# Ten engine loops of a four-layer graph network written out with constants

## What is computed

```python
h = relu(layernorm(x)); x = x + L0(h)
h = relu(layernorm(x)); x = x + L1(h)
h = relu(layernorm(x)); x = x + L2(h)
h = relu(layernorm(x)); x = x + L3(h)

L0: clip(h + segment_sum(h[src] * edge_prob * weight, dst) + 0.1 * h, 0, 1)
L1: segment_sum(sum_k t[:, k] * (h[dst] @ W1[k]), src)       # 16 basis terms of edge_attr_2
L2: segment_sum(h'[src] . (edge_attr_8 @ We + be), dst) + h' @ Wr + b, and the same with the
    edges turned round; 8 + 8 columns
L3: a = segment_sum(silu(h[dst] x edge_attr_8 . Wmsg) @ Wlin, src)
    h + silu(h x a . Wupd) @ Wul
```

## Time and profile before

| | |
|---|---|
| median of 3 runs | 4584.79 us (4582.91 to 4585.53) |
| the profiled execution | 4580.59 us, span 4578.8 us |
| PE, PE's weight loads | 2142.2 us busy (47%), 1442.9 us (32%) |
| DVE | 2888.0 us (63%) |
| ACT | 1181.5 us (26%) |
| POOL | 2834.2 us (62%) |
| DMA | 319.82 MB, mean 70 GB/s |
| granted TensorE clock, mean | 0.716 |

### The profile page before, as it was taken

How to read it: one execution, slowest core, us unless ns; L and a number is a source line. 1 busy time by engine, 2 the same in 40 slices (tenths; PEclk the granted TensorE clock), 3 DMA queues, 4 the chain that set the end, 5 groups by cost and what they waited for, 6 DMA issues and landing times.

```text
span 4578.8 us, 36295 instructions
## 1 busy us (share of the span) xinstructions
PE 2142.2 (47%) x6770; PEld 1442.9 (32%) x6770; DVE 2888.0 (63%) x4329; ACT 1181.5 (26%) x2942; POOL 2834.2 (62%) x2799
## 2 busy tenths in 40 slices
PE   1200015555200005666666126666660566666998
PEld 0100014444200003333333115555550344433444
DVE  8890026666460006777777777777776688876887
ACT  1010013333310003333333234444341344431111
POOL 4877777777777776555554036555530677773776
PEclk7555557777655557888888657777775788888999
DMA  6010013333530002222224212222243233352110
GB/s 167 7 47 24 8 38 105 110 104 111 83 97 5 5 5 52 72 72 72 72 72 71 90 63 85 83 84 76 83 80 114 82 108 100 106 84 65 32 32 24
DMA packets 200402, 319.82 MB, mean 70 GB/s; under 512 B 83898, under 2 KB 166698, under 8 KB 199971
## 3 DMA queue, kind: packets, MB, share of 16 engines
q1 hardware_dynamic: 112848, 265.61, 16.3%
q0 software_dynamic: 82368, 21.64, 7.5%
q10 hardware_dynamic: 5140, 32.09, 1.8%
HBM read 66.90 MB, written 252.21 MB: 70 GB/s over the span
## 4 chain that ended last, share of the span: by engine, by line
PE 22%; DVE 19%; issue 10%; POOL 6%; DMA 2%; SPq 2%; DVEq 1%; ACT 0%; POOLq 0%
DVE work L1122 9%; PE psX L562 8%; PE psX L651 7%; POOL rows L464 5%; PE psK L553 4%; DVE psX L1152 2%; PE psX L578 2%; DVE natD L1147 2%; DMA rows<-table,rec 1%; DVEq L1122 1%; DVE work L1104 1%; SPq L407 1%; SPq L408 1%; PE psK L628 1%; DVE at_hi L1099 1%
## 5 line engine op out<-in xcount | busy, mean ns | idle before, releaser
L464 POOL DMA_INDIRECT rows<-table,rec x1792 | 1692.6, 945 | 1268.0 <-issue 528.4
L553 PE MATMUL psK<-work 128*128 128x224 f32 x3584 | 927.7, 424 | 648.8 <-DVE work L1104 374.4
L553 PEld LDWEIGHTS psK<-work 128*128 128x128 f32 x3584 | 848.1, 241 | 819.3 <-issue 501.8
L1122 DVE SCALAR_TENSOR_TENSOR work<-work,keep,psK 128x224 f32<-128x224 f32 x1792 | 799.8, 446 | 233.7 <-DVE work L1122 45.2
L562 PE MATMUL psX<-natD 128*128 128x512 f32 (+1 forms) x1120 | 682.7, 750 | 535.6 <-DVE natD L1147 257.2
L749 ACT ACTIVATE work<-iota,rec 128x128 f32<-128x128 f32 x1792 | 546.0, 391 | 641.3 <-PE psK L553 360.2
L446 POOL DMA_INDIRECT edges_by_dst<-natD,pos x391 | 440.4, 1126 | 184.1 <-issue 126.7
L562 PEld LDWEIGHTS psX<-natD 128*128 128x128 f32 x1120 | 258.0, 254 | 800.1 <-DVE natD L1147 329.7
L446 POOL DMA_INDIRECT edges_by_src<-natS,pos x391 | 403.5, 1032 | 127.2 <-issue 127.2
L1104 DVE TENSOR_TENSOR work<-at_hi,psX 128x1792 f32<-128x1792 f32 x224 | 452.3, 2019 | 6.1 <-ACT psX L791 0.3
L589 PE MATMUL psX<-ident,rows 128*128 128x128 f32 x168 | 51.9, 309 | 803.9 <-DMA rows<-table,rec 803.9
(11 more groups left out here) (142 smaller groups left out, 2068.0 us busy)
## 6 DMA issues: line engine op xcount, KB each, us to landing
scan<-work SPq DMA_DIRECT2D x224, 896.0 KB, 3.6
rows<-table,rec POOLq DMA_INDIRECT x1792
table<-h ACTq DMA_DIRECT2D x28, 896.0 KB, 3.6
work<-scan SPq DMA_DIRECT2D x168, 112.0 KB, 2.0
rec<-edges_by_dst SPq DMA_DIRECT2D x112, 84.0 KB, 1.9
natD<-scan SPq DMA_DIRECT2D x56, 112.0 KB, 2.0
edges_by_dst<-natD,pos POOLq DMA_INDIRECT x391, 2.1
edges_by_src<-natS,pos POOLq DMA_INDIRECT x391
```

The source lines that it names most:

```text
L464: pool.indirect_dma_start(out=rows[k][:, u * D:(u + 1) * D], out_offset=None, in_=table.ap(), in_offset=bass.IndirectOffsetOnAxis(ap=rec[k ...
L553: nc.tensor.matmul(psK[:, o:o + BW], at_lo[par][:, t * P:(t + 1) * P], spread[par][:, t * BW:(t + 1) * BW], start=True, stop=True)\
L1122: V.scalar_tensor_tensor(acc[par][:, t * BW:(t + 1) * BW], was, keep[s][:, bass.ds(q * G + t, 1)], psK[:, o:o + BW], ALU.mult, ALU.add).th ...
```

## The change

The ten loops become Python loops: each turn is emitted with its own constants, in the same order on each engine. Register arithmetic, counters and branches of these loops go, waits and addresses become constants, and the increments of `pool_go` and `sp_go` go with their semaphores. The value loaded in L407 stays a register.

```diff
-        pool_go = sem("pool_go")
-        sp_go = sem("sp_go")
...
                         sp.wait_ge(e["spread"], g + 1)
-                        sp.sem_inc(sp_go, 1)
                         sp.wait_ge(e["lo"], g + 1)
...
-                    with sp.Fori(0, ROUNDS - 2) as i:
+                    for i in range(0, ROUNDS - 2):
...
-                        with sp.Fori(0, PER) as j:
+                        for j in range(0, PER):
                             t = sp.value_load(last[s][0:1, bass.ds(j + c * PER, 1)], min_val=0, max_val=T - 1)
...
                     pool.wait_ge(rec_in[k], i * 16 + (PAST_REC[l] + 16))
-                    pool.sem_inc(pool_go, 1)
                     if not first:
                         pool.wait_ge(used, i * RING + (k - RING + 1))
-                        pool.sem_inc(pool_go, 1)
...
-                with pool.Fori(1, ROUNDS) as i:
+                for i in range(1, ROUNDS):
...
                 pool.wait_ge(up["moved"], c + 1)
-                pool.sem_inc(pool_go, 1)
                 pool.wait_ge(up["resid"], c + 1)
-                pool.sem_inc(pool_go, 1)
...
-            with pool.Fori(1, NCH) as c:
+            for c in range(1, NCH):
...
-                with pe.Fori(1, ROUNDS) as i:
+                for i in range(1, ROUNDS):
...
-            with pe.Fori(1, NCH - 1) as c:
+            for c in range(1, NCH - 1):
...
-                with act.Fori(1, ROUNDS) as i:
+                for i in range(1, ROUNDS):
...
-            with act.Fori(1, NCH - 1) as c:
+            for c in range(1, NCH - 1):
...
-                with dve.Fori(1, ROUNDS) as i:
+                for i in range(1, ROUNDS):
...
-            with dve.Fori(1, NCH) as c:
+            for c in range(1, NCH):
```

## The result

The changed kernel takes 4447.6 us (median of 4 runs, 4443.2 to 4450.4) against 4583.9 before: a ratio of 0.971, 95% interval 0.969 to 0.972. The forecast was 4475, in the range 4445 to 4510. So 136 us were gained where 110 had been added up.

The account below looks back on a forecast made before the run. No engine above 63% busy: DVE, with waits for PE, paces layers 1 and 2, POOL layers 0 and 3. Terms 41.8 + 35.4 + 7 + 6.4 + 14.6 + 3.6 + 1.4 = 110.2 us off 4584.8 give 4475, range 4445 to 4510.

Parts of the forecast that it names:

- DVE behind its waits: Layers 1 and 2: run()'s register instruction behind each wait is DVE idle time, 0.68 us a looped group; 41.8 + 35.4 us.
- a tail of 0.5: Ends of edge stages, a last run() behind the last gather: 0.68 in layer 3, as much in layers 1 and 2; 1.4 us.
- the edges of the loop in layer 1: Layer 1, from run()'s end to the first L1147: 3.1 us for 39 groups, 3.3 us for 13 where the loop turns.
- The clock: PE's products 2 and 3: shorter idle time makes 2.4 GHz likelier, 0.1 a group in layer 2, 0.03 in layer 1; 7 us.
- Rival 2: The clock holds: PE keeps 2.4 GHz for products 2 and 3 in layer 2, 50 us more, 4425; chance 0.06.
- What root() hides: Layer 2: root()'s two adds behind run() hide the remaining loop costs, so only run()'s 35.4 us counts.
- The loads: SP's loads between layers: constants save 0.45 or 0.35 us a load; 6.4, 14.6 and 3.6 us before layer 2, layer 3, update.
- Layers 0 and 3 at POOL's pace: Layers 0 and 3: POOL's gathers 1.25 us apart cover what DVE, PE, ACT and SP lose there; put at nothing.
- Rival 1: Written-out code stalls on instruction fetch: 4645, chance 0.03; weaker form, DVE alone, 38 us, 4513, chance 0.07.
- Rival 3: Something else takes the place, or loops cost only their turns (6.5 us): no change, 4578 to 4585; chance 0.02.

Follow-up runs that it names:

- the one address: Kernel before, loops kept, but run() takes its factor from a constant column of keep instead of a register address: 5030.8 us, ratio 0.989.
- the addresses ahead of the loads: Changed kernel with SP's register loads of a chunk's eight addresses moved ahead of that chunk's waits and DMAs: 4430.1 us, ratio 0.967.
- the two loops alone: Kernel before with only DVE's loop over the groups and SP's over a chunk's loads written out: 4979.7 against 5084.7 us, ratio 0.979.

## Why the prediction was right, and where its sizes were off

**DVE behind its waits (41.8 + 35.4 us): right, cause and size, but for the edges.** Layer 1 gave 44.1, where 41.8, the clock's 1.6 and a tail of 0.5 stood; run() in layer 2 gave 35.0. The cause, the address behind the wait, was put to the test by the one address. PE did follow DVE. The 6.4 us for the edges of the loop in layer 1 are right in the sum only: with the edges left in and the one address made constant, layer 1 gained the same 43.6 us in 52 groups, so they aren't shown to be a gain of their own.

**The clock (7 us): right in kind, too small in layer 2.** The term that was mis-sized is "I take 0.1 a group in layer 2", 5.2 us, where the waits for PE fell by 11.8, or 0.23 a group. Two steps led to it. "The bounds are 0 and 2.29 - 1.23 = 1.06 a group, 55 us a layer" counts products 2 and 3, but not the root products behind them, which run at the same clock: a group at the high level is some 1.9 us shorter. And the peeled groups with their full wait were taken as typical, while six of the 52 groups got the whole and eleven a part. PE's idle time in front of product 2 did not come to 2.56 everywhere: it is 3.29 in the second group above, 1.65 in the first and 2.77 in the mean. Rival 2 (the clock holds in layer 2, 4425) stayed a rival: it came to pass in a few of the 52 groups.

**What root() hides.** "Behind them stand root()'s two adds, which hide the rest" was wrong for the turns of the loop: 2.4 us ahead of L1099 were put at nothing and were gained. With run()'s 35.0 and the waits' 11.8 this is 49.2 of layer 2's 49.8 us.

**The loads (24.6 us): right in place, an eighth short.** "I leave 0.05, and take 0.45 off a load of the first chunk and 0.35 off the later ones" was 0.61 and 0.40; the waits gave 7.6, 15.8 and 4.7 us, 28.1 in all, where 6.4, 14.6 and 3.6 stood. The update gave 1.8 more in PE's first transposes (8.1 us to the first DVE instruction before, 6.3 after), and that comes and goes: it is 8.1 with the addresses ahead of the loads and 6.3 with the two loops alone.

**Layers 0 and 3 at POOL's pace: right.** The gathers are as far apart as before. Of the 7.1 us of layer 3 only 0.5 were in the sum; 6.1 are the tail that no loop explains.

**The range.** 4447.6 lies 2.6 us above its lower edge. Of the 21 us by which the profiled pair beats the sum, 8.7 are layer 2's, 7.7 lie in the two node stages and the update, and 6.6 in layer 3; 2.1 were lost ahead of layer 1.

**Rival 1, instruction fetch: not there.** 1.3 MB more were fetched, and most of DVE's instructions of run() stand 35 ns apart: 16.4 us idle for 416 of them in layer 2. The waits of `place(1)` come to the same total, 127.2 us before and 127.3 now in the page's row of L443, so they were not what the rival priced. The Trainium skill, Runtime: NRT & Kernel Launch, Instruction fetch mechanics, has it that straight-line code mostly hides its fetches; the traces agree.

**Rival 3**, that the loops cost no more than their turns, fell with the address: its 6.5 us would have been the whole gain, and with every turn of the loop left in, layer 1's step fell from 14.47 to 13.63 us.

## What to carry to other kernels

Look for register instructions that stand behind a wait for the same engine's instruction before: each of them is idle time, even at 46 ns, while the counters and the registers for waits, which DVE's queue worked out ahead, cost nothing that showed here. In layer 1 one address made constant gave what the written-out loop gave. And where a short chain waits for PE behind its own idle time, price all that runs at the lower clock and that the other engine waits for, not the first part of it, and try keeping PE busy: here it was worth 148 us, more than the whole change (132 on the same chip).

## What the runs showed that I had not expected

- Matmuls whose result nobody reads, 8 a group in layer 1 and 6 in layer 2, made the kernel 148 us faster (4449.8 to 4301.6), since PE then had 2.4 GHz for the ones that DVE waits for.
- The same kernel takes 4582 us on one chip and 5085 to 5092 on another, with the same instructions; in one trace from there DVE waits 638 us in 85 waits ahead of run(), most of them where it waits for no store, and the cause is open.
- SP's loop over loads ran at 1.49 us a turn and not 1.71 once the other loops were written out, its own code unchanged.
